# Ranks inside the next block's aggregation, place ahead of the norm, and the second chunk's rows gathered ahead of the first chunk's weights

## The reference, cut to what matters

```python
h = layernorm(x) @ W.T + b                        # 1250 x 1024
deg = edges that start in a node                  # of 20000 edges and one loop per node
norm = deg[row] ** -0.5 * deg[col] ** -0.5
x1 = x + segment_sum(norm[:, None] * h[col], row) # aggregation and residual
x2 = layernorm(x1)
logits = x2 @ router_w.T + router_b               # 8 experts
vals, ids = top_k(logits, 2); w = softmax(vals)
y = sum over the two chosen experts e of
      w[e] * (gelu(x2 @ w1[e].T + b1[e]) @ w2[e].T + b2[e])   # hidden width 512
out = x1 + (layernorm(x2 + y) * ln_w + ln_b)
```

## Time and profile before

| | us |
|---|---|
| median of 3 runs | 670.1 (669.8 to 671.56) |
| profiled execution | 669.16 |
| its span in the profile | 667.1 |
| PE busy | 568.5 (85% of the span) |
| DVE busy | 486.9 (73%) |
| ACT busy | 247.8 (37%) |
| POOL busy | 206.3 (31%) |
| mean granted clock of PE | 0.934 of full speed |

### The profile page before, as it was taken

How to read it: one execution, slowest core, us unless ns; L and a number is a source line. 1 busy time by engine, 2 the same in 40 slices (tenths; PEclk the granted TensorE clock), 3 DMA queues, 4 the chain that set the end, 5 groups by cost and what they waited for, 6 DMA issues and landing times.

```text
span 667.1 us, 13061 instructions
## 1 busy us (share of the span) xinstructions
PE 568.5 (85%) x3944; PEld 319.8 (48%) x3945; DVE 486.9 (73%) x1301; ACT 247.8 (37%) x374; POOL 206.3 (31%) x200
## 2 busy tenths in 40 slices
PE   0598999989999999999496999999999989999300
PEld 0243455545454455555383565656565656565100
DVE  8998967886416588888877869686868691574297
ACT  4332433323327033434442443444444440321470
POOL 2740000000000116556536343544444441041130
PEclk9999999999979999999597999999999996999755
DMA  5694000000002723444755788878887885053978
GB/s 204 221 366 179 3 1 1 1 1 2 2 2 91 283 100 127 172 146 158 217 171 189 193 269 210 279 203 276 205 283 192 267 211 189 0 102 126 235 221 262
DMA packets 35052, 106.16 MB, mean 159 GB/s; under 512 B 8978, under 2 KB 9391, under 8 KB 34992
## 3 DMA queue, kind: packets, MB, share of 16 engines
q1 hardware_dynamic: 24912, 73.86, 29.8%
q0 software_dynamic: 8896, 27.38, 19.5%
q10 hardware_dynamic: 1184, 4.20, 2.1%
HBM read 71.75 MB, written 33.67 MB: 158 GB/s over the span
## 4 chain that ended last, share of the span: by engine, by line
PE 72%; DVE 19%; issue 3%; DMA 2%; ACT 2%; DVEq 1%; POOL 0%; POOLq 0%; ACTq 0%; SPq 0%
PE ps L1747 6%; PE ps L1748 6%; PE ps L1883 6%; PE ps L1884 6%; PE ps L1885 6%; PE ps L1843 5%; PE ps L1844 5%; PE ps L1845 5%; PE ps L1671 4%; PE ps L1672 4%; PE ps L1673 4%; PE ps L1825 3%; PE ps L1598 3%; PE ps L1617 3%; DVE wbufs L1149 2%
## 5 line engine op out<-in xcount | busy, mean ns | idle before, releaser
L606 POOL DMA_INDIRECT acc_rows<-work,ids_out x24 | 52.2, 2176 | 120.3 <-DVE work L1472 120.3
L513 POOL TENSOR_TENSOR work<-work 128x1024 f16<-128x1024 f32 x9 | 19.2, 2132 | 223.0 <-ACT work L872 223.0
L1747 PE MATMUL ps<-wbufs,rows_and_counts 128*128 128x512 f16 x200 | 75.8, 379 | 0.5 <-DVE wbufs L1252 0.5
L1843 PE MATMUL ps<-rows_and_counts,wbufs 128*128 128x336 f16 (+1 forms) x256 | 75.1, 299 | 0.8 <-DVE rows_and_counts L1410 0.8
L1748 PE MATMUL ps<-wbufs,rows_and_counts 128*128 128x512 f16 x200 | 75.8, 379 | 0.0
L1844 PE MATMUL ps<-rows_and_counts,wbufs 128*128 128x336 f16 (+1 forms) x256 | 75.1, 299 | 0.0
L1845 PE MATMUL ps<-rows_and_counts,wbufs 128*128 128x336 f16 (+1 forms) x256 | 75.1, 299 | 0.0
L1883 PE MATMUL ps<-wbufs,rows_and_counts 128*128 x192 | 73.6, 383 | 1.6 <-issue 1.3
L1425 DVE SCALAR_TENSOR_TENSOR wbufs<-stage,wbufs 128x1024 f16<-128x1024 f32 x56 | 67.2, 1218 | 9.2 <-ACT wbufs L899 9.0
L1884 PE MATMUL ps<-wbufs,rows_and_counts 128*128 x192 | 73.3, 382 | 0.0
L1885 PE MATMUL ps<-wbufs,rows_and_counts 128*128 x192 | 73.3, 382 | 0.0
(11 more groups left out here) (311 smaller groups left out, 1156.6 us busy)
## 6 DMA issues: line engine op xcount, KB each, us to landing
stage<-wst_in SPq DMA_DIRECT2D x72, 512.0 KB, 5.8
acc_rows<-work SPq DMA_DIRECT2D x10, 512.0 KB
x_rows<-work SPq DMA_DIRECT2D x10, 512.0 KB
t<-x_in SPq DMA_DIRECT2D x1, 4096.0 KB, 14.1
wbufs<-b_in ACTq DMA_DIRECT2D x8, 512.0 KB
wbufs<-acc_rows SPq DMA_DIRECT2D x8, 512.0 KB, 5.9
t<-x_in SPq DMA_DIRECT2D x1, 3072.0 KB, 10.2
t<-x_in SPq DMA_DIRECT2D x1, 2048.0 KB, 7.8
```

The costliest lines, as they stand in the source:

```text
L1747: mm(o, ct_hi[:, cs], hs[:, at:at + HALF], start=(m == 0), stop=False, skip_group_check=True)
L1843: mm(o, wbufs[:, ds(w + ws, P)], x_hi, start=(j == 0), stop=False)
```

## The change

It has four parts, and computes the same numbers.

1. `rank(r - 2)` is issued inside `aggregate(r, 1)`, behind its matmuls of block m = RANK_AT = 7 (the loop runs over m = 0 to 9), for r = 2 to 9. `rank(8)` and `rank(9)` stay at the ends of iterations 10 and 11. On DVE `place(r - 2)` follows `choose(r - 2)` directly and so stands ahead of `add_agg(r)`; in iteration 10 it stands ahead of `x2t_lo(9)`, in iteration 11 ahead of `first_turned(0)`.
2. POOL: behind the third tile's gather (which has a semaphore of its own now, `third_in`) come the slot numbers of chunk 1, read into another buffer, `ids_weights`, and the gathers of its rows. They wait for the slot table, for the chunk list and for the first two tiles. The gathers of chunk 0's weights follow. `chunk(0)` then waits for the third tile and the weights. Semaphore counts of the third tile are 16 lower everywhere.
3. POOL's two `add_lnb` are removed. DVE does them: `add_lnb(0)` in chunk 0 of expert 0, block 7 at expert 1, blocks 8 and 9 at expert 6.
4. DVE: the nine instructions of `plans` stand ahead of the eight `turned(0, j)`, and `weights_of(0)` moves into chunk 0, behind `turned(1, 0)` and `turned(1, 1)`.

```diff
--- before.py
+++ after.py
@@ -73,6 +73,7 @@
 FIRST_TILES = 7
 PLAN = 32
 EARLY = 4
+RANK_AT = 7
 W2AT = DK * FF
 WB = 2 * PIECES * D
 LO = PIECES * D
@@ -425,6 +426,7 @@
         y_ready_b2 = sem("y_ready_b2")
         carrier = sem("carrier")
         gathered = [sem(f"gathered{i}") for i in range(CT)]
+        third_in = sem("third_in")
         added = [sem(f"added{i}") for i in range(CT)]
         extra_done = sem("extra_done")
         extra_used = sem("extra_used")
@@ -512,15 +514,10 @@
                 pool.wait_ge(xs_hi_done, m + 1)
                 g.tensor_tensor(xs[:, D:], xn, xs[:, 0:D], ALU.subtract).then_inc(xs_done, 1)
 
-            def add_lnb(r):
-                rs = slice(r * D, (r + 1) * D)
-                pool.wait_ge(xn_done, NT + r + 1)
-                g.tensor_tensor(t[:, rs], t[:, rs], b_row[:], ALU.add).then_inc(x1b_done, 1)
-
             def gather_first(i, ids, tiles):
                 g.indirect_dma_start(out=gx0[i], out_offset=None, in_=x2_rows[0:CH + tiles * P, :],
                                      in_offset=bass.IndirectOffsetOnAxis(ap=ids[:, i:i + 1].bitcast(U32), axis=0)
-                                     ).then_inc(gathered[i], 16)
+                                     ).then_inc(gathered[i] if i in FIRST else third_in, 16)
 
             pool.wait_ge(lnb_in, 16)
             pool.wait_ge(consts_in, 16 * 5)
@@ -552,7 +549,7 @@
                                          in_offset=bass.IndirectOffsetOnAxis(ap=ids[:, i:i + 1].bitcast(U32), axis=0)
                                          ).then_inc(cw_in, 16)
 
-            def gather(rows):
+            def gather(rows, ids=ids):
                 for i in range(CT):
                     g.indirect_dma_start(out=rows[i], out_offset=None, in_=x2_rows,
                                          in_offset=bass.IndirectOffsetOnAxis(ap=ids[:, i:i + 1].bitcast(U32), axis=0)
@@ -568,22 +565,21 @@
             pool.wait_ge(ids_in, 2 * 16)
             for i in range(len(FIRST), CT):
                 gather_first(i, ids, NT)
+            pool.wait_ge(table_loaded, 16)
+            pool.wait_ge(chunks_done, 1)
+            for i in FIRST:
+                pool.wait_ge(gathered[i], 16)
+            st4.enter(0)
+            chunk_ids(1, ids_weights)
+            gather(gx, ids_weights)
             pool.wait_ge(cw_stored, 16)
             gather_weights(ids)
-            pool.wait_ge(table_loaded, 16)
-            pool.wait_ge(chunks_done, 1)
             c_last = pool.value_load(last_chunk[:], min_val=NE - 1, max_val=MAXC - 3)
 
             def chunk(c, ahead=None, last=False):
                 if isinstance(c, int):
-                    st4.enter(0)
-                    for i in range(CT):
-                        pool.wait_ge(gathered[i], 16)
+                    pool.wait_ge(third_in, 16)
                     pool.wait_ge(cw_in, 16 * CT)
-                    chunk_ids(1, ids)
-                    gather(gx)
-                    add_lnb(NT - 2)
-                    add_lnb(NT - 1)
                     chunk_ids(0, ids_out)
                 else:
                     st4.enter(3 * c if last else 3 * c + 1)
@@ -595,7 +591,7 @@
                     chunk_ids(c, ids_out)
                 if ahead is not None:
                     for i in range(CT):
-                        pool.wait_ge(gathered[i], 16 * c + 32)
+                        pool.wait_ge(gathered[i], 16 * c + (32 if i in FIRST else 16))
                     pool.wait_ge(x4_done, DK * c + DK)
                     settle(pool)
                     chunk_ids(c + 2, ids)
@@ -1341,17 +1337,16 @@
             for r in range(NT + 2):
                 if 2 <= r:
                     choose(r - 2)
+                    if r == NT + 1:
+                        st3.wait()
+                        v.engine_nop().then_inc(gap_done, 1)
+                    place(r - 2)
                 if r == NT + 1:
                     first_turned(0)
                 if r < NT:
                     add_agg(r)
                 if r == NT:
                     x2t_lo(r - 1)
-                if r == NT + 1:
-                    st3.wait()
-                    v.engine_nop().then_inc(gap_done, 1)
-                if 2 <= r:
-                    place(r - 2)
 
             dve.wait_ge(gap_exp, 1)
             st3.link(v.tensor_scalar(wt[:, NT:], gap_e[:], 1.0, None, ALU.add))
@@ -1429,10 +1424,6 @@
                 first_turned(j)
                 if j >= DK - EARLY:
                     piece_lo(0, j - (DK - EARLY), (e_hi[1], e_lo[1]))
-            for j in range(DK):
-                turned(0, j, FIRST_CH)
-            weights_of(0)
-
             st3.link(v.tensor_scalar(plans_f[:], ranges2_f[:, 0, :], float(PLAN), None, ALU.mult))
             st3.link(v.tensor_tensor(plans_f[:], plans_f[:], ranges2_f[:, 1, :], ALU.add))
             st3.link(v.tensor_scalar(plans_f[:], plans_f[:], 4.0, None, ALU.mult))
@@ -1442,6 +1433,9 @@
             st3.did(v.tensor_scalar(chunk_ups, chunk_ups, float(FK), None, ALU.max))
             st3.link(v.tensor_scalar(chunk_downs, chunk_downs, float(PIECES), float(FK), ALU.mult, ALU.max))
             v.tensor_copy(plans[:], plans_f[:]).then_inc(plans_done, 1)
+
+            for j in range(DK):
+                turned(0, j, FIRST_CH)
 
             def chunk(c, e, h, split, first=False, last=False):
                 st4.enter(c * LINKS4)
@@ -1456,8 +1450,7 @@
                 if not last:
                     turned(c + 1, 0)
                     turned(c + 1, 1)
-                if not first:
-                    weights_of(c)
+                weights_of(c)
                 dve.wait_ge(cw_copied, c + 1)
                 dve.wait_ge(rows_added, c + 1)
                 for i in range(CT):
@@ -1480,9 +1473,9 @@
                     return
                 dve.wait_ge(y_ready, c * CT + CT)
                 v.tensor_copy(hold[:, 1:2], hold[:, 0:1]).then_inc(y_ready_b2, 1)
-                if split is not None and not first:
+                if split is not None:
                     add_lnb(e)
-                    for r, at in ((0, 1), (NT - 3, NE - 2)):
+                    for r, at in ((NT - 3, 1), (NT - 2, NE - 2), (NT - 1, NE - 2)):
                         if isinstance(e, int) and e == at:
                             add_lnb(r)
 
@@ -1735,7 +1728,7 @@
                 linear(NT - 1, quarter, xt_ps)
 
 
-            def aggregate(r, n):
+            def aggregate(r, n, ranked=None):
                 o = agg_ps[r % 2][:, n * HALF:(n + 1) * HALF]
                 if r >= 2:
                     pe.wait_ge(var_done, len(NORM_GROUPS) + r - 1)
@@ -1746,6 +1739,8 @@
                         pe.wait_ge(hs_lo_done, m + 1)
                     mm(o, ct_hi[:, cs], hs[:, at:at + HALF], start=(m == 0), stop=False, skip_group_check=True)
                     mm(o, ct_hi[:, cs], hs[:, D + at:D + at + HALF], start=False, stop=False, skip_group_check=True)
+                    if ranked is not None and m == RANK_AT:
+                        rank(ranked)
                 with pe.If(big):
                     for m in range(NT):
                         cs = slice(m * NP + r * P, m * NP + (r + 1) * P)
@@ -1789,7 +1784,7 @@
 
                 for i in tiles:
                     if j == 0:
-                        pe.wait_ge(gathered[i], 16)
+                        pe.wait_ge(gathered[i] if i in FIRST else third_in, 16)
                     for h in range(2):
                         ins = mm(x4_ps[j % 2][:, i * P:(i + 1) * P],
                                  gx0[i].bitcast(F16)[:, h * D + j * P:h * D + (j + 1) * P],
@@ -1803,13 +1798,13 @@
                 if r >= 2:
                     route(r - 2)
                 if r < NT:
-                    aggregate(r, 1)
+                    aggregate(r, 1, r - 2 if r >= 2 else None)
                 if 1 <= r <= NT:
                     turn2(r - 1)
                 if r == NT + 1:
                     for j in range(2):
                         turn_first(j, FIRST).then_inc(first_done, 1)
-                if r >= 2:
+                if r >= NT:
                     rank(r - 2)
 
 
@@ -1819,7 +1814,7 @@
                 pe.wait_ge(x4_lo_done, c * DK + (j + 1))
                 for i in range(CT):
                     if j == 0:
-                        pe.wait_ge(gathered[i], c * 16 + 16)
+                        pe.wait_ge(gathered[i], c * 16 + (16 if i in FIRST else 0))
                     for h in range(2):
                         at = c % 2 * (2 * CT * D) + ((2 * i + h) * D + j * P)
                         ins = mm(x4_ps[j % 2][:, i * P:(i + 1) * P], rows16[:, ds(at, P)], ident16[:],
```

## The result

The changed kernel takes 674.03 us (median of 16 runs, 671.25 to 676.77) against 669.92 for the kernel before (16 runs, 667.18 to 671.56). The ratio is 1.0064, with a 95% interval of 1.0049 to 1.008: **slower by 0.64%, or 4.3 us** (4.1 between the two medians), where 669.1 and "no change" was forecast. The profiled execution took 674.1, its span is 672.3, 5.2 more than before.

A forecast was written before the change was run, and what follows sets the result against it. PE was taken to bound the loop and expert chunks, but not the 50 us between. 0.9 + 4.1 - 0.4 + 0.5 - 6.1 = -1.0 us, from the median 670.1 to 669.1 ("no change"); range 666.0 to 674.6.

The forecast's parts named there:

- unexplained 1.88 us: Chunk 0: pause before three gelus, taken to stay; if it went too, the gain would be 7.7 instead of 6.1.
- The loop, +0.9: Block loop: each norm 1.3 to 1.4 us later, mostly hidden by PE's aggregation; 0.9 lost over eight blocks (0.5 to 1.9).
- The tail, +4.1: Last two blocks: later transposes, DVE's 7.85 us list and a 1.8 hold start the first expert 4.1 us later.
- L1311 would start under it and be held: Tail: place(8)'s product starts at about 325.9 under POOL's subtraction and is held till 327.8, costing 1.8 us.
- Up-first at the lower clock, -0.4: First expert's matmuls: part of the lower-clock time may pass before they start, giving 0.4 us (bounds -0.9 and +0.9).
- Plans, +0.5: Nine small DVE instructions moved ahead of turned(0,0) fill DVE's idle and overrun it: 0.5 us lost (0.3 to 0.8).
- Chunk 0, -6.1: Chunk 0: earlier rows and unheld casts end the first down result at 358.8, not 364.9: 6.1 us gained (3.1 to 7.7).
- what then bounds is ACT's gelu: Chunk 0 after the change: gelus until 356.30, casts until 358.1, three matmuls, so the first down result ends at 358.8.
- rival C: Chunk 0: PE stays at the lower clock while waiting for casts, gain only 3.1, time 672.1; chance 0.10.
- B: Loop: routing masks fall under POOL's subtraction, rank holds PE 0.85 us in each of seven blocks, 675.1; chance 0.13.
- D: Chunk 0: chunk 1's rows still land at 357 or later, gain 0.7 in place of 6.1, 674.5; chance 0.07.
- A: Tail or chunk 0: POOL's hold is missed or the gelu pause goes, 667.4 (both 665.6); chance 0.20.

The follow-up runs named there:

- group 2: Four kernels on one chip: changed kernel again 673.5 us, with chunk 1's gathers held 676.19, with POOL's last weight subtraction cut 670.62, with the old gather order 673.94.
- bias_only: Part 3 alone on the kernel before (POOL's two bias additions go to DVE): 669.54 us, ratio 1.0004.
- groups 1, 3, 4 and 5: Fourteen kernels on three other chips: parts of the change, single orders restored, weight loads held or POOL's last subtraction cut; medians 662.78 to 674.58 us.
- rows_held: Changed kernel with POOL's gathers of chunk 1's rows held until ACT's last first-expert copy: 676.19 us, ratio 1.0094 to the kernel before.
- ranks_bias_plans: Parts 1, 3 and 4 without 2 (chunk 1's gathers in the old order and place): 673.94 us, ratio 1.0068 to the kernel before.
- x2t_first: Changed kernel with x2t_lo(9) ahead of place(8) again: 666.95 us, ratio 0.9966 to the kernel before.
- no_ranks: Parts 2, 3 and 4 on the kernel before, ranks as before: 664.11 us, ratio 0.9927.
- group 5: Runs on the fourth chip, including the changed kernel with POOL's last weight subtraction cut, without and with second-expert weight loads held: 666.99 and 666.06 us.
- stage_held: Changed kernel with SyncE's loads of the second expert's weights held until ACT's eight third-tile copies: 667.5 us, ratio 0.9965 to the kernel before; repeat 668.54.
- loop_only: Part 1 on the kernel before for blocks 0 to 7 only, last two iterations and all else as before: 671.31 us, ratio 1.0022.
- old_tail: Changed kernel with DVE's old order in the last two iterations: 666.06 us, ratio 0.9959 to the kernel before.
- ranks_only: Part 1 alone on the kernel before (ranks inside the aggregation, place ahead of the norm): 674.58 us, ratio 1.0066.
- free_held: Changed kernel with POOL's last weight subtraction cut to 8 columns and SyncE's second-expert weight loads held: 666.06 us, ratio 0.9948 to the kernel before.
- after_again: The changed kernel run once more, unaltered: 673.5 us, ratio 1.0049 to the kernel before.
- plans_back: Parts 2, 3 and 4 with the nine plan instructions behind the turned copies again, ranks as before: 662.78 us, ratio 0.9891 to the kernel before.

## Why the prediction was wrong

- **The sum.** The parts add up to -0.5 where both were measured, near the forecast of -1.0. What failed first is a term that stands nowhere in it. The prediction books each hand-over from PE at the recorded end of its matmul ("the transposes end 1.4 later, at 325.3", "route(9) 0.7", the gelus behind `up`). In the changed kernel's profile PE's signals came late: 2.11 us behind the last recorded start for route(8), 2.8 for the first expert's last transposes and 2.0 for a gelu, where the median is 0.23. Each of the twelve "remote" idles of the five profiles that have any, the changed kernel's and the four of group 2, ends with a semaphore that PE raises, 1.8 to 2.8 us behind its matmul's recorded start. In the changed kernel they cost 2.0 us ahead of the first expert and 3 to 4.2 from there to the first down result (33.9 against 29.7 and 30.9 with the same program).
- **A row ahead of the result showed it.** The "unexplained 1.88 us" before three gelus of the earlier trace rows is the same thing: `up`'s last three matmuls with a signal stand at 352.48, 352.98 and 353.49, and their signals at 354.68 to 354.88. Bias_only, with the same program up to there, has no such pause. The kernel before loses nothing by it that its rows show: PE waits for gathered rows until 356.97 anyway, and DVE is held until 358.98. So of the twenty profiles six have late signals between 316 and 374 (before, the changed kernel, the four of group 2), and the fourteen of groups 1, 3, 4 and 5 none over 0.7 us. The six also have only 5,773 to 5,920 records of semaphores, the others 6,344 to 6,351; where such a record is missing a signal can look late, but those named here are followed at once by the engine that waited.
- **What makes PE's signals late stays open**, and so does whether PE itself ran later than its records say. The order of the gathers alone is not it (rows_held and ranks_bias_plans have it), nor a busy DMA alone: its share was 1.00 over the 2.8 us that the changed kernel's ACT waited for L1789, but 0.88 and 0.93 in the same place in x2t_first and no_ranks. All of group 2 has it, and none of the profiles from the other three chips. The changed kernel was not timed on those. An estimate from group 5: stage_held and its repeat (667.5, 668.54) plus the 0.9 that holding the loads gave gives 668.4 to 669.4, beside 669.4 to 670.2 for the kernel before, that is no change, as forecast.
- **The loop, +0.9.** Right as far as it can be told. The norm's shift is there (place at 283.00 of the forecast 283.1), and the transposes of block 9 start 2.0 later, which leaves 0.6 for waits beside 1.4 of shift. Over all profiles route(8)'s last matmul stands at 321.5 in mean with the old loop (six) and 323.7 with the new (fourteen), each with a spread of some 2.4. Loop_only and old_tail price it at 1.5 and 2.0 with the shift; loop_only's interval reaches to 0.
- **The tail, +4.1.** Right in ranks_only: 9.66 us from the transposes to the first expert against 9.65, and 7.6 in free_held, without the hold, against 7.85. That the first agrees to 0.01 is luck: the hold was 0.2 longer and the rest 0.2 shorter. In the changed kernel's own runs it is 11.6, and the step that failed there is "L1311 would start under it and be held": choose(8) came 1.5 us late, so POOL's subtraction held the cast ahead of rank(8) and place(8), and not place(8)'s product. The hold has about the same price in both places, 2.0 to 2.2.
- **Up-first at the lower clock, -0.4.** Right in its sign, and too small. From its first to its last matmul's end the first expert took 14.9 us before and 13.8 in ranks_only and both profiles of stage_held, which start at 335.7 to 337.4, so 1.1 less; the low bound was 0.9. In the changed kernel's profile it took 18.1 (14.2 in after_again): PE's wait for ACT's late copy (2.2) and the lower clock behind it (0.66 from 352 to 357) cover the gain.
- **Plans, +0.5.** Right: from the first expert's end to up(0)'s end takes 8.5 in no_ranks and 8.0 in plans_back and before.
- **Chunk 0, -6.1.** Too large. The step that failed is "what then bounds is ACT's gelu", with the casts behind it: PE's own chain was longer. It had 1.86 us of its own instructions between up(0) and L1818, hidden before under the wait for rows, and it made six of the twelve down matmuls at the lower clock, some 1.2 us more. Together, 3.1, they cover the 2.5 by which no_ranks' result came late. The second is rival C; my argument against it, that the clock had held through pauses from 345.6 to 351.5, was no argument. What it gave back is 3.1 against the profile of before and 5.4 against bias_only, so the size hangs on which execution without it is taken.
- **Rivals B and D** did not come: the masks' cast is at 0.17 in the loop, PE never waits for rows at L1820, and rank never stops PE there. A did not come in the changed kernel.
- **The range.** Its low end is "all low ends gives -5.8"; they add up to -5.5 with 0.5 for the loop. Nothing else hangs on it. That 674.0 still lies inside the range is luck: C and B held it open to 674.6, and the time came by neither alone.

The skill's rule from the prediction (the Trainium skill, "GPSIMD Engine Reference", § 8 "Key points") has the trace on its side at a further place: two small plan instructions took 2.18 and 2.27 under POOL's additions, one with a single SBUF source. L1304 never stood under a running subtraction, so its case stays untested.

## What to carry to other kernels

When a wait is taken away, list what its engine still has to do between the two instructions (its own register work, a lower clock) before booking the whole wait as gain. A reordering that is nearly neutral where PE is the bound costs in the last iterations, where nothing covers it (9.1 us from route(8) to the first expert in old_tail, 12.2 in ranks_only): peel these off and keep their order, as old_tail and plans_back do. When a profile names a releaser that the kernel cannot have, look up which engine raises the semaphore that the line waits for; and a pause in the profile of before that nothing explains should be looked for in a second profile before a forecast is built on it. And run a change's parts beside the whole on one chip; a sum of parts that differs from the whole is a finding about the runs as much as about the kernel.

## What the runs showed that I had not expected

- A VectorE instruction that starts ahead of POOL's is held too, not only one that starts under it: 2.23 us from 326.54, with POOL's subtraction from 326.61 (ranks_only), and, in the earlier trace rows already, L1455 for 5.54 us from 353.44 with POOL's additions from 353.90, 0.46 later.
- A matmul's semaphore can come 1.8 to 2.8 us behind its recorded start, and the profile then calls the idle of the engine that waits "remote" on a program of one core.
- The same program differed by 3.6 us between two chips (670.62 and 666.99) while the kernel before, beside it, differed by 0.7 (670.05 and 669.38).
